# A mixture-of-experts layer between two attention layers: token rows moved by gathers and scatters in the experts, with lists inverted on TensorE

## What is computed

```python
# x: normed tokens, N = 4096 rows of D = 256; E = 8 experts; k = 2
C = k * int(1.25 * ((N + E - 1) // E))                  # 1280 slots an expert
scores = softmax(x @ wg);  gates, idx = top_k(scores, 2)
gates = gates / clip(sum(gates), EPS)
loc_sel = ...   # place of the token in its expert's queue: a cumulative sum over tokens
keep = loc_sel < C
gates = gates * keep
pos = where(keep, idx * C + loc_sel, E * C)             # token -> slot
buf[pos] = x                                            # each token's row into its two slots
h = silu(einsum('ecd,ehd->ech', disp, fc1_w) + fc1_b)
y = einsum('ech,ehd->ecd', h, fc2_w) + fc2_b
combined = sum over the two choices of gates * ybuf[pos]
res = hidden_states + combined
out = layernorm(res) * ln_gamma + ln_beta               # then x = x + tanh(g) * out
```

## Time and profile before

| | before |
|---|---|
| three runs | 2028.10, 2028.48, 2030.90 us (median 2028.48) |
| the profiled execution | 2028.7 us, of which its span is 2027.0 |
| mean clock granted to PE | 0.863 of full speed |
| busy: PE, DVE, ACT, POOL | 1549.9, 1271.1, 927.0, 677.9 us |
| instructions | 30246 |
| read from DRAM, written | 122.6 MB, 93.2 MB |
| POOL's DMA queue (software), SP's (hardware) | 89.2 MB, 127.8 MB |

### The profile page before, as it was taken

One profiled execution on the slowest core, in us unless ns is written; L12 is line 12 of the kernel. 1 busy time (PEld: TensorE's weight loads), 2 busy tenths in 40 slices (PEclk: granted clock), 3 DMA queues, 4 the chain that ended last, 5 costly groups with the idle time before them and its releaser, 6 DMA issues. The chain is left out here.

```text
span 2027.0 us, 30246 instructions
## 1 busy us (share of the span) xinstructions
PE 1549.9 (76%) x11862; PEld 1033.1 (51%) x11863; DVE 1271.1 (63%) x1934; ACT 927.0 (46%) x1235; POOL 677.9 (33%) x913
## 2 busy tenths in 40 slices
PE   2877369999996820399999999934539999997734
PEld 2766323333333720399999999932213333332522
DVE  2544289999982450255555555338839999995457
ACT  1333138888882111144444444411106888886104
POOL 0211026555532327300000000038613555540457
PEclk9988669999997855699999999976668999999765
DMA  7565565555534032122123221113353655552002
GB/s 216 185 187 184 172 113 136 132 134 131 142 93 189 40 112 101 62 82 94 45 88 91 87 79 51 42 52 109 124 136 86 135 133 139 135 133 66 0 0 83
DMA packets 131982, 218.89 MB, mean 108 GB/s; under 512 B 28912, under 2 KB 77104, under 8 KB 130688
## 3 DMA queue, kind: packets, MB, share of 16 engines
q1 hardware_dynamic: 97600, 127.77, 21.2%
q0 software_dynamic: 34240, 89.18, 17.2%
HBM read 122.61 MB, written 93.21 MB: 106 GB/s over the span
## 5 line engine op out<-in xcount | busy, mean ns | idle before, releaser
L881 DVE TENSOR_REDUCE a_nmax<-a_ring 128x2 f32<-128x1024 f32 x512 | 608.6, 1220 | 37.5 <-PE a_ring L792 37.2
L864 ACT ACTIVATE a_pexp<-a_ring 128x1024 f32<-128x1024 f32 x512 | 522.8, 1027 | 201.7 <-PE a_ring L802 201.5
L816 PE MATMUL a_pout<-a_pexp,a_v 128*17 128x256 f32 x4096 | 321.5, 387 | 0.7 <-ACT a_pexp L864 0.7
L792 PE MATMUL a_ring<-a_k,a_q 64*128 64x512 f32 x1024 | 243.5, 474 | 74.9 <-DMA a_q<-qs 65.1
L802 PE MATMUL a_ring<-a_q,a_k 64*128 64x512 f32 x1024 | 258.9, 502 | 5.4 <-DVE a_nmax L881 4.5
L1420 ACT ACTIVATE e_full<-e_pH,b1T 128x256 f32<-128x256 f32 x320 | 133.8, 469 | 258.4 <-PE e_pH L1380 258.3
L802 PEld LDWEIGHTS a_ring<-a_q,a_k 64*128 64x128 f32 x1024 | 96.4, 185 | 228.6 <-DVE a_nmax L881 137.6
L1449 DVE TENSOR_TENSOR e_hid_lo<-e_full,e_hid_hi 128x512 fp32r<-128x512 f32 x160 | 110.6, 691 | 156.1 <-ACT e_hid_hi L1428 156.1
L1399 PE MATMUL e_pY<-fc_w_hi,e_hid_hi 128*128 128x256 f32 x640 | 184.3, 288 | 0.2 <-DVE e_hid_lo L1449 0.2
L1380 PE MATMUL e_pH<-e_rowsT_hi,fc_w1T_hi 128*128 128x256 f32 x640 | 181.9, 284 | 1.5 <-DVE e_rowsT_lo L1286 1.5
L1380 PE MATMUL e_pH<-e_rowsT_lo,fc_w1T_hi 128*128 128x256 f32 x640 | 181.7, 284 | 0.0
(11 more groups left out here) (259 smaller groups left out, 2527.4 us busy)
## 6 DMA issues: line engine op xcount, KB each, us to landing
outs<-a_osb SPq DMA_DIRECT2D x64, 256.0 KB, 2.8
fc_raw<-in_L_ffn_fc_w SPq DMA_DIRECT2D x16, 1024.0 KB, 8.2
a_k<-ks POOLq DMA_DIRECT2D x112, 128.0 KB, 3.3
a_q<-qs POOLq DMA_DIRECT2D x112, 128.0 KB, 3.5
disp<-r_zeros SPq DMA_DIRECT2D x8, 1280.0 KB, 13.7
vs<-p_va SPq DMA_DIRECT2D x16, 544.0 KB, 10.4
a_v<-vs POOLq DMA_DIRECT2D x16, 544.0 KB, 5.3
ks<-p_parts_k_hi SPq DMA_DIRECT2D x32, 256.0 KB
```

Source lines behind the costliest of these rows:

```text
L792: mm = e.matmul(max_bank(m)[:, hh, :], q[j][at, p, t * P:(t + 1) * P], k[j][at, p, :], start=True, stop=True)
L816: mm = e.matmul(pout[n % 2][32 * h:32 * h + VW, at], v[b % 2][:, t, g * HG + h, :], pexp[t][:, h, at], start=(t == 0 and half == 0), stop= ...
L864: e.activation(pexp[t][:, 2 * p:2 * p + 2, :], score_bank(n * U + i)[:, :, :], ACT.Exp).then_inc(exped, 1)
L881: e.tensor_reduce(nmax[n % 2][:, :].rearrange("p (x y t) -> p x y t", x=2, y=2)[:, :, p, t], max_bank(m)[:, :, :], AX.X, ALU.max, negate=T ...
```

## The change

The direction of the moves is turned round. Instead of every token writing its row into two slots ahead of the experts, and fetching two results behind them, each chunk of the experts gathers the rows of its 256 slots, and scatters its 256 results to rows that are ordered by token.

- For this the token-to-slot lists are inverted. The place in the expert is split into `c1` (in units of 128) and `c0` (the rest). `key` is expert * 10 + c1 + 1, or 0 for a dropped token. For each of 64 (choice, tile) pairs DVE compares the numbers 0 to 127 with c0 (`c0_hot`, 128 x 128) and the numbers 1 to 80 with key, times the tile's number (`key_hot`, 128 x 80), and once a quarter makes a second half of key_hot that holds the partition's number. PE adds up the 64 products c0_hot^T * key_hot in PSUM: entry (c0, key) is then the tile and the partition of the one token in that slot. DVE makes of these `slot_get` and `slot_put`, 128 x 80 each. An empty slot reads some token's row and writes to a scratch row.
- route: SP stores the normed rows to `normed` (8 DMAs of 512 KB, `kept`), and clears 8 MB of `ytok` instead of 10 MB of disp and the rows of ybuf.
- place: the 64 indirect writes, their copies by ACT and lists by DVE are gone. ACT rounds the first expert's weights (`take_fc1_high`, `cut_fc2_high`), DVE makes the remainder of fc1 (one a quarter), POOL that of fc2 and the scaled gamma and beta. PE's products of the quarters stand behind its turns of fc1.
- experts: POOL issues 2 indirect reads a chunk (two chunks ahead, behind `trr`), in the first eight chunks adds beta to 4 tiles of X (`shifted`), and behind `ye` issues 2 indirect writes to ytok. SP's loads of rows and POOL's plain stores are gone.
- combine: the lists and the 64 indirect reads are replaced by 16 plain loads from POOL's queue, 512 KB each.

```diff
@@ place, vector @@
...
+                for qq in range(QUARTERS):
+                    kk, j = qq // 2, qq % 2
+                    if qq >= 2:
+                        e.wait_ge(slotted, qq - 1)
+                    for m in range(QT):
+                        t = qq % 2 * QT + m
+                        e.tensor_scalar(c0_hot[j][:, m, :], countb[:, :], c0[:, kk, t:t + 1], None, ALU.is_equal).then_inc(marked, 1)
+                        e.tensor_scalar(key_hot[j][:, m, 0, :], countb[:, 1:SLOTS + 1], key[:, kk, t:t + 1],
+                                        float(kk * NT + t + 1), ALU.is_equal, ALU.mult).then_inc(marked, 1)
+                    e.wait_ge(marked, (qq + 1) * 2 * QT)
+                    e.tensor_scalar(key_hot[j][:, :, 1, :], key_hot[j][:, :, 0, :], 0.0, partition[:, 0:1],
+                                    ALU.is_gt, ALU.mult).then_inc(built, 1)
+                    S.fc.take_fc1_low(e, 0, 0, qq)
...
+                e.wait_ge(slotted, QUARTERS)
+                e.tensor_copy(held[:, :], pS[:, 0, :]).then_inc(c.up(), 1)
...
@@ place, tensor @@
                 for w in range(S.fc.GROUPS):
                     S.fc.turn_fc1(e, 0, 0, w)
+                for qq in range(QUARTERS):
+                    e.wait_ge(built, qq + 1)
+                    for m in range(QT):
+                        last = e.matmul(pS[:, :, :].rearrange("p s c -> p (s c)"), c0_hot[qq % 2][:, m, :],
+                                        key_hot[qq % 2][:, m, :, :].rearrange("p s c -> p (s c)"),
+                                        start=(qq == 0 and m == 0), stop=(qq == QUARTERS - 1 and m == QT - 1))
+                    last.then_inc(slotted, 1)
@@ place, gpsimd @@
-                @loop(e, B // SET)
-                def _(i):
-                    for j in range(SET):
...
-                                e.indirect_dma_start(S.disp[:, :], bass.IndirectOffsetOnAxis(ap=at[j][:, kk, t:t + 1], axis=0),
-                                                     rows[j][:, t, :], None).then_inc(put[j], 16)
+                for w in ("gamma_b", "beta_b"):
+                    e.tensor_scalar(S.w[w][:, :], S.w[w][:, :], S.tg[:, 2:3], None, ALU.mult).then_inc(scaled, 1)
+                for w in range(S.fc.GROUPS):
+                    S.fc.cut_fc2_low(e, 0, 0, w)
@@ ExpertWeights @@
+    def take_fc1_high(self, e, n, x, w):
+        m, k, j0 = n * self.GROUPS + w, w // 2, (w % 2) * 4
+        e.wait_ge(self.trw, m + 1)
+        if m:
+            e.wait_ge(self.wte, 2 * m)
+        e.activation(self.w1T[x][HI][:, k, j0 * P:(j0 + 4) * P], self.pw[w % 2][:, :, :], ACT.Copy).then_inc(self.wte, 1)
+
+    def cut_fc2_low(self, e, n, x, w):
+        m, at = n * self.GROUPS + w, slice(2 * w, 2 * w + 2)
+        e.wait_ge(self.w2e, 2 * m + 1)
+        e.tensor_tensor(self.w2[x][LO][:, at, :], self.raw2[:, at, :], self.w2[x][HI][:, at, :], ALU.subtract).then_inc(self.w2e, 1)
@@ experts, gpsimd @@
-                        e.dma_start(S.ybuf[ds(m * CHUNK, CHUNK), :].rearrange("(t p) d -> p t d", p=P), y[mi % 2][:, :, :]
-                                    ).then_inc(yst[mi % 2], 16)
+                def gather_rows(m):
+                    for t in range(2):
+                        c = m * 2 + t
+                        e.indirect_dma_start(rows[m % 2][:, t, :], None, S.normed[:, :],
+                                             bass.IndirectOffsetOnAxis(ap=S.slot_get[:, c:c + 1], axis=0)).then_inc(ldr[m % 2], 16)
+
+                gather_rows(0)
+                gather_rows(1)
+                for m in range(E * NCH):
+                    if m + 2 < E * NCH:
+                        e.wait_ge(trr, m + 1)
+                        gather_rows(m + 2)
+                    if m < B:
+                        x = S.X[:, tiles(m), :]
+                        e.tensor_tensor(x, x, over_tiles(S.w["beta_b"]), ALU.add).then_inc(shifted, 1)
+                    e.wait_ge(ye, m + 1)
+                    for t in range(2):
+                        c = m * 2 + t
+                        e.indirect_dma_start(S.ytok[:, :], bass.IndirectOffsetOnAxis(ap=S.slot_put[:, c:c + 1], axis=0),
+                                             y[m % 2][:, t, :], None).then_inc(yst[m % 2], 16)
@@ combine, gpsimd @@
-                def gather(j):
...
+                def load_rows(b):
+                    if b >= 2:
+                        e.wait_ge(added, (b - 1) * ADDS)
                     for kk in range(2):
+                        first = E * CAP + kk * N + b * SEQ
+                        e.dma_start(yg[b % 2][:, kk, :, :], S.ytok[first:first + SEQ, :].rearrange("(t p) d -> p t d", p=P)
+                                    ).then_inc(got[b % 2][kk], 16)
```

More of the change, by code:

```diff
@@ L1005, in _ @@
                 e.wait_ge(zeroed, 1)
-                e.dma_start(S.ybuf[E * CAP:E * CAP + P, :], zeros[:, 0, :]).then_inc(cleared, 16)
                 for b in range(B):
-                    e.dma_start(S.disp[b * ZROWS * P:(b + 1) * ZROWS * P, :].rearrange("(p r) d -> p r d", p=P),
+                    e.dma_start(S.ytok[E * CAP + b * ZROWS * P:E * CAP + (b + 1) * ZROWS * P, :].rearrange("(p r) d -> p r d", p=P),
                                 zeros[:, :, :]).then_inc(cleared, 16)
-                e.wait_ge(cleared, 16 * (B + 1))
+                for b in range(B):
+                    nb.wait(e, b)
+                    e.dma_start(S.normed[b * SEQ:(b + 1) * SEQ, :].rearrange("(t p) d -> p t d", p=P),
+                                S.BIG[:, tiles(b), :]).then_inc(kept, 16)
+                e.wait_ge(cleared, 16 * B)
+                e.wait_ge(kept, 16 * B)
             @block.gpsimd
@@ new lines, in _ @@
+                e.scalar_tensor_tensor(out=lost[:, :], in0=held[:, :], scalar=0.0, in1=other[:, 0:SLOTS],
+                                       op0=ALU.is_equal, op1=ALU.mult).then_inc(c.up(), 1)
+                e.tensor_scalar(second[:, :], held[:, :], float(NT), -float(N), ALU.is_gt, ALU.mult).then_inc(c.up(), 1)
+                e.scalar_tensor_tensor(out=spare[:, :], in0=held[:, :], scalar=0.0, in1=unused[:, :],
+                                       op0=ALU.is_equal, op1=ALU.mult).then_inc(c.up(), 1)
@@ L1174, in _ @@
                 e.wait_ge(c.sem, c.k)
-                e.tensor_scalar(S.row_get[:, :, :], t3[:, :, :], float(E * CAP), None, ALU.add).then_inc(c.up(), 1)
-                e.wait_ge(sp, 1)
-                e.tensor_tensor(t4[:, :, :], pos[:, :, :], spare[:, :, :], ALU.subtract).then_inc(c.up(), 1)
+                e.tensor_tensor(lost[:, :], lost[:, :], second[:, :], ALU.add).then_inc(c.up(), 1)
+                e.scalar_tensor_tensor(out=S.slot_put[:, :], in0=token[:, :], scalar=float(E * CAP - P), in1=spare[:, :],
+                                       op0=ALU.add, op1=ALU.add).then_inc(c.up(), 1)
@@ L1192, in _ @@
[L1192 to L1201 removed]
+                e.scalar_tensor_tensor(out=S.slot_get[:, :], in0=token[:, :], scalar=-float(P), in1=lost[:, :],
+                                       op0=ALU.add, op1=ALU.add).then_inc(c.up(), 1)
```

179 lines of the change are left out of this document (76 added, 103 removed).

## The result

The changed kernel took **1964.2 us** (median of 4 runs, 1958.9 to 1970.2) against 2029.7 before: a ratio of **0.967, 95% interval 0.963 to 0.971**. The forecast was 1958.5 with 1943 to 1980. The profiled execution took 1959.7 us with a span of 1957.7, so 69.3 us less span than before; the forecast's sum, made against the profiled execution, was 70.2 less.

The account below looks back on a forecast made before the run. POOL's 64 indirect writes bound placement, PE the experts, no engine combine. First transpose -56.3, seam to combine +3.1, combine -17.0: -70.2 against 2028.7, and 0.2 less for the median, given as 1958.5 us; range 1943 to 1980.

Parts of the forecast that it names:

- Route, 0: Route stage: SP's added stores of the normed rows cost nothing; 5.3 us if their cover were gone.
- Table: Placement: 64 compare pairs at 0.38 us, 24.3, plus long operations, fc1 remainders, standstill and tail; last list at 781.9.
- just under cover: Placement: ACT and POOL cut fc2 in turns from about 770, 7.6 us, ending at 778, hidden beside the table.
- the rule that I had put against the change: Placement: POOL and DVE block each other; a POOL issue of 0.96 us became 8.29 under one DVE operation.
- rival B: Placement: table dear, 0.52 us a pair, and POOL's four cuts hold DVE 1.2 each; 1973.9 us, chance 0.15.
- Seam to the experts, 4.7: Last list to PE's first transpose: 0.3 seam, 0.4 and 2.2 for two gathers, 1.8 landing; transpose at 786.6, -56.3.
- Experts. Cost 0: Experts: POOL's gathers, scatters and additions to X fit its 11.2 us of idle time per 11.94 us chunk; cost 0.
- Seam to combine, +3.1: Experts to combine: last result in two indirect writes +1.5, longer seam after an indirect write +1.6; lower bound 1.5.
- Combine, -17.0: Combine: first X -9.5, shorter rstd waits -3.8, shorter waits for stores of qs -3.7; bounds -13.3 and -21.
- A's cheap table: Placement, rival: a compare pair costs 0.21 us, in proportion to its elements; 10.9 less, 1947.6 us, chance 0.14.
- C's point: Experts, rival: POOL becomes the bound from 3.0 us an issue, blocked by DVE's subtractions; 2056 us at 3.6, chance 0.03.
- D: Seam to the experts, rival: they did not wait for the scatter, so removing it changes nothing; 2028 us, chance 0.01.

Follow-up runs that it names:

- fc2 on DVE: Changed kernel with the four fc2 remainders moved from POOL into DVE's standstill in the placement, ACT making the high parts first: 1968.2 us, ratio 0.968.
- X on DVE: Changed kernel with the eight additions of beta to X moved from POOL to DVE, ahead of its wait for the down product: 1967.3 us, ratio 0.969.
- the second measurement: The changed kernel run once more without edits, as base for the other runs: 1975.2 us, ratio 0.971 to the kernel before.
- the early gathers: Changed kernel with all edits, the second expert's fc2 loaded after the first rows landed, and gathers issued ahead of the scatters: 1950.1 us, ratio 0.961.

## Why the prediction was right, and where its steps were not

The forecast's sum was right to 1.7 us against the profiled execution (-68.5 at attention's start for -70.2), but by terms that cancel: an error of +11.0 in the experts met 4.1 us ahead of them, 0.6 at the seam and 4.6 in combine that came better than forecast. That they met is luck. In the prediction's total is also a slip: 2028.7 - 70.2 is 1958.5 already, and 0.2 less for the median is 1958.3.

- *Route, 0*: right; placement began at 720.96 (722.17 in the earlier trace rows), inside the spread of that stretch.
- *Table*: a pair took 0.31 instead of 0.38 (16 pairs in 5.0 us), -4.2; long operations 0.6 each instead of 1.05, -1.8; PE's products 0.14 instead of 0.20, so standstill 3.3 instead of 4.5 and tail 2.35 instead of 3.2; the start 1.2 earlier. With the small operations behind them, all this is 9.0 us less; only the sizes were off.
- *"just under cover"*: wrong, and it is the rule that I had put against the change. POOL's four cuts did end in time, but each held a table operation for 1.0 us, +4.2 in all. The Trainium skill (SBUF — State Buffer, "SBUF: two separate sides") says that a GpSimd instruction that reads SBUF and a DVE one in a 2-port mode or with two SBUF inputs exclude each other for the whole instruction; the compare at 764.59 (1.26 us for 0.24) and the e_hid_lo of two SBUF tiles at 805.48 (3.35 for 0.69) agree, and the addition of the earlier trace rows has two SBUF inputs too. I gave this to rival B alone, although 8.29 us in the earlier trace rows spoke for it. Without it the last list would have come at 773 rather than 777.1; with fc2 on DVE it did come 4.2 earlier.
- *Seam to the experts, 4.7*: 5.4 (1.05 to the first issue, 2.4 for two, 1.9 landing). -60.4 in all for -56.3.
- *"Experts. Cost 0"*: **the step that failed, +11.0.** I costed POOL's additions by POOL's idle time and asked only whether POOL would be late. The question was whom POOL holds: e_hid_lo of two SBUF tiles, on which PE waits. The first sum came 0.5 us later, the first seven intervals between sums grew from 86.3 to 96.8 us together, the others not at all; with X on DVE the 1.5 us a chunk are gone. The average 2.35 of the earlier trace rows told nothing of this, since it is POOL's own duration. The prediction had named this as a sign of being wrong, that PE idles between chunks, and it came true: PE waited eight times for e_hid_lo, 9.0 us. Its chunk of 11.94 us was read from the last ones alone; before the change most take 12.38.
- *Seam to combine, +3.1*: +2.5.
- *Combine, -17.0*: -21.6, just beyond its bound of -21. First X came 11.6 us into combine for 13.3, since the loads landed at 4.4 and 5.9 rather than 5.6 and 8. ACT's waits for the stores of qs fell from 10.4 to 8.7 on average, none above 9.9 for 12.51 in the earlier trace rows; of the two cases I had left open, it was the one in which loads do not slow the stores.
- *Rivals*: A's cheap table came true in part, and B's held operations too, at once; C's point (3 us an issue) was never near, an issue took 0.94 to 1.36 us and 0.3 to the next; D is excluded. But C asked a question that 0.17 us a gather answers otherwise than I had: hidden issues are not free.

The median lies 5.7 us above the forecast. Against the median of before from the same measurement it is 65.5 us less, and two of the four executions lie near 1970. In the second measurement the experts are 7.6 us longer than in the first profile; why is open.

## What to carry to other kernels

An operation that moves to an engine with idle time should be costed by whom it blocks, not by that idle time: an addition of two SBUF tiles on POOL cost PE 1.5 us a chunk, on DVE in its own idle time nothing. Ask of a large load which small transfers on the path go out just behind it. When terms cancel, the total proves none of them; the stages of the profile have to be compared one by one.

## What the runs showed of the hardware

- POOL and DVE: while POOL subtracted or added two SBUF tiles (1.26 or 2.39 us), a DVE compare of 0.24 us took 1.26 and a DVE subtraction of 0.69 took 3.35.
- A bf16 compare with a scalar per partition, 128 or 80 elements, lasts 0.24 us in the median, and the next starts 0.16 us behind the start of the larger and 0.15 behind that of the smaller.
- A load of 1 MB on SP's queue, issued between two 128-row gathers of POOL's, had the rows land 4.5 us behind the second issue; issued once the rows had landed, it left 1.8.
- Beside 128-row gathers in combine, ACT waited 72.8 us for the stores of qs, beside plain loads 60.3. The cause is open.
- With indirect gathers right behind indirect scatters, ACT was released late by PE's products (6.1 us behind an output sum for 5.76, about every fifth chunk 6.8) in all eight profiles of such kernels on two chips. It was not in either profile with only one kind, not with the gathers ahead of the scatters on a third chip, and not in the first profile of the changed kernel. The trace names no cause. Whether the time of issue or the number of transfers decides stays open; it would take the early gathers on one of those two chips.
